# Causal 16-head attention: second passes laid out by halves of the queries

## The reference, cut to what matters

```
x = x + _L1_attn_ref(_layernorm(x), W_Q, W_K, W_V, W_O)

B, S, _ = x.shape                                  # 4, 1024
Q, K, V = (proj(W_Q), proj(W_K), proj(W_V))        # (B, 16, S, 8): heads of 8
Q = _apply_rope(Q, cos, sin); K = _apply_rope(K, cos, sin)
scores = einsum('bhsd,bhtd->bhst', Q, K) / sqrt(8)
scores = where(tril(ones((S, S))), scores, -inf)   # causal
out = einsum('bhst,bhtd->bhsd', softmax(scores), V)
return einsum('bsd,ed->bse', out.transpose(0, 2, 1, 3).reshape(B, S, 128), W_O)
```

## Time and profile before

| | |
|---|---|
| median of three runs | 5018.72 us |
| profiled execution, own time | 5018.88 us |
| its span, first to last instruction | 5017.5 us |
| PE, DVE, ACT, POOL busy, share of the span | 93%, 86%, 66%, 58% |
| mean granted TensorE clock | 0.969 of 2.4 GHz |
| causal stage, first to last maximum | 3851.6 to 4399.7 us |

### The profile page before, as it was taken

One profiled execution on the slowest core, in us unless ns is written; L12 is line 12 of the kernel. 1 busy time (PEld: TensorE's weight loads), 2 busy tenths in 40 slices (PEclk: granted clock), 3 DMA queues, 4 the chain that ended last, 5 costly groups with the idle time before them and its releaser, 6 DMA issues.

```text
span 5017.5 us, 149633 instructions
## 1 busy us (share of the span) xinstructions
PE 4665.0 (93%) x62728; PEld 3234.6 (64%) x62728; DVE 4324.5 (86%) x8627; ACT 3291.3 (66%) x6490; POOL 2930.2 (58%) x3101
## 2 busy tenths in 40 slices
PE   6999997999999999999999999999996999989978
PEld 3444444777777777777777777777775555545467
DVE  7989997999999999999999999999986777768566
ACT  4888884666666666666666666666663777756632
POOL 1330305778877887788778777877872222016744
PEclk7999998999999999999999999999997999989989
DMA  0000100000000000000000000000000000000000
GB/s 25 2 2 1 34 6 25 23 10 12 13 27 11 12 13 27 10 13 14 26 13 16 13 27 11 12 13 10 8 5 27 2 2 2 2 17 1 1 1 18
DMA packets 51764, 63.72 MB, mean 13 GB/s; under 512 B 12820, under 2 KB 41258, under 8 KB 50322
## 3 DMA queue, kind: packets, MB, share of 16 engines
q1 hardware_dynamic: 51090, 54.14, 3.6%
HBM read 25.17 MB, written 4.19 MB: 6 GB/s over the span
## 4 chain that ended last, share of the span: by engine, by line
PE 54%; DVE 26%; ACT 9%; issue 8%; POOL 3%; DMA 0%; SPq 0%; DVEq 0%; POOLq 0%; ACTq 0%
PE psum L582 7%; PE psum L1182 6%; PE psum L1244 6%; PE psum L551 5%; PE psum L1227 4%; PE psum L1259 3%; DVE a_top L731 3%; PE psum L1191 3%; PE psum L1299 3%; DVE b_cross L1498 3%; DVE b_stat L1537 3%; PE psum L568 2%; DVE x L1531 2%; DVE x L1494 2%; DVE b_prob_t L1550 1%
## 5 line engine op out<-in xcount | busy, mean ns | idle before, releaser
L1651 POOL TENSOR_TENSOR x<-x,b_cross 128x512 f32<-128x512 f32 x768 | 984.4, 1285 | 58.3 <-DVE b_cross L1498 58.3
L1657 POOL TENSOR_TENSOR x<-x,b_norm 128x512 f32<-128x512 f32 x768 | 788.3, 1046 | 206.9 <-ACT b_norm L1338 206.0
L1259 PE MATMUL psum<-b_w_vo,b_mixed 128*128 128x128 f32 x6144 | 779.1, 275 | 0.3 <-issue 0.3
L1259 PEld LDWEIGHTS psum<-b_w_vo,b_mixed 128*128 128x128 f32 x6144 | 753.4, 192 | 26.8 <-issue 0.4
L731 DVE TENSOR_REDUCE a_top<-psum 128x2 f32<-128x1024 f32 x512 | 604.1, 1218 | 64.8 <-PE psum L551 61.1
L665 ACT ACTIVATE a_prob<-psum 128x512 f32<-128x512 f32 x1024 | 543.3, 598 | 60.1 <-PE psum L568 46.3
L1664 POOL TENSOR_TENSOR x<-x,b_stat 128x512 f32<-128x512 f32 x384 | 397.5, 1048 | 309.4 <-DVE b_stat L1542 309.0
L1331 ACT ACTIVATE b_square<-psum 128x512 f32<-128x512 f32 x768 | 462.6, 602 | 143.8 <-PE psum L1182 120.7
L1494 DVE TENSOR_TENSOR x<-psum,b_table 128x512 f32<-128x512 f32 x768 | 515.6, 671 | 16.3 <-ACT b_square L1331 15.6
L1380 ACT COPY b_mixed<-psum 128x512 f32<-128x512 f32 x768 | 439.6, 601 | 137.1 <-PE psum L1244 137.0
L1498 DVE TENSOR_TENSOR b_cross<-psum,b_table 128x512 f32<-128x512 f32 x768 | 521.9, 679 | 0.0
(11 more groups left out here) (354 smaller groups left out, 10678.5 us busy)
## 6 DMA issues: line engine op xcount, KB each, us to landing
b_prev<-b_xs_x SPq DMA_DIRECT2D x24, 384.0 KB
ab<-in_L_ffn_Wqkv SPq DMA_DIRECT2D x6, 1024.0 KB, 5.0
b_shifted_x<-y SPq DMA_DIRECT2D x24, 224.0 KB
b_shifted_f<-y SPq DMA_DIRECT2D x48, 112.0 KB, 2.1
ab<-in_L_ffn_Wqkv SPq DMA_DIRECT2D x6, 512.0 KB, 6.0
ab<-in_L_ffn_Wo SPq DMA_DIRECT2D x6, 512.0 KB, 7.3
b_prev<-b_xs_x SPq DMA_DIRECT2D x24, 112.0 KB
x<-in_L_attn_x SPq DMA_DIRECT2D x4, 512.0 KB, 6.5
```

What stands on the lines that cost most here:

```text
L1259: made = e.matmul(banks[n][:, 0:D], mixed[:, h, :], w_vo[l % 2][:, h, :], start=h == 0, stop=h == 2 * PAIRS - 1)
L1651: e.tensor_tensor(turned, turned, crossing, ALU.add).then_inc(sem["roped"], 1)
L1657: e.tensor_tensor(rh, rh, bcast(norm[i % 2][:, 1, HPC * c:HPC * (c + 1)], 2, LDIM), ALU.mult).then_inc(sem["scaled"], 1)
```

## The change

In the causal stage `parts` becomes CHUNKS = 2, as it is in the other attention stage.

```diff
@@ mha_order
-    parts = 1 if causal else CHUNKS
+    parts = CHUNKS
     each, chunks = TILES // parts, CHUNKS // parts
```

## The result

The changed kernel takes 5083.93 us (median of 4 runs, 5080.39 to 5090.21), the kernel before 5020.4 us on the same chips: a ratio of 1.0133, 95% interval 1.0121 to 1.0145. It is slower by 64 us where 11 us less was forecast, and lies outside the range. The profiled execution, the slowest of the four, took 5090.2 us; its span is 71.1 us longer than before.

The account below looks back on a forecast made before the run. No engine was simply full: in-order PE waits for banks that DVE or ACT hold, the limit varying by slots. Head -1.1, tail -9 and units -1.4 took 5018.9 to 5007.4 us; range 4992 to 5030.

Parts of the forecast that it names:

- that the stage's clock stays as it was: Causal stage's steady units: priced at full granted clock; a fall there was given no size or chance.
- The prediction's own sign of being wrong: Causal stage: wrong if a plain unit is below 31.3 or above 33 us, or the steady clock falls.
- plain unit: 24 causal-stage slots with norms and projections elsewhere: forecast -0.25 us, to 32.05 us.
- Slots 8 to 15, +1.25 us: Second third of each unit: all four seconds groups become 512 wide; 12.0 us, ends 11.4 and 13.6.
- Slots 16 to 23, -1.35: Last third of each unit: narrow groups replace 512-wide ones; 10.05 us in place of 11.42, ends 9.1 and 11.4.
- Slots 0 to 7, -0.15: First third of each unit: same pairs, a turn_q2 leaves and a turn_back comes; -0.15 us.
- Head, -1.1: Start of causal stage: slots 22 to 29 gain seconds beside firsts, 11.0 us in place of 12.1.
- The assumption on the clock: Head: clock rises 9 us after seconds begin, wherever that is; if it stays at 3902.0 instead, +3 us.
- Tail, -9: After the last first: 8 slots of seconds alone drop out; -9 us, ends -13 and -7.
- Shift operations, 0: Each unit: three more on DVE, +0.4 us covered by idle time in slots 8 to 10; uncovered, 6 us.
- The ACT rival: ACT bounds slots 8 to 15 at 13.6 us, plain unit 34.7; slower, 5043 us; chance 0.20.

Follow-up runs that it names:

- e1: Changed kernel, groups of c = 1 reordered to k = 4 to 7, then 0 to 3, restoring the old seconds-to-firsts pairing with the 22-slot lag; 5021.5 us, 1.0017.
- e12: Changed kernel, DVE's 512-column maxima in slots 16 to 23 taken over only the first 256 columns; 5028.74 us, 1.0021.
- e10: e1 with the groups of c = 0 in the order k = 0, 3, 2, 1; 5026.67 us, 1.0014.
- e11: e10 with turn_q2 of the first half at slot 18 in place of 12; 5022.09 us, 1.0007.
- e2: Changed kernel with its halves and two shifts a unit, but seconds back at the old lag of 30 slots; 5021.05 us, 1.0006.
- e3: Changed kernel with the score matmuls of firsts in slots 16, 17, 20, 21 issued twice; 5103.77 us, 1.0158.
- e6: Changed kernel with a whole-array identity transpose ahead of firsts in slots 16, 17, 20, 21 and every other first in slots 0 to 7; 5145.32 us, 1.0249.

## Why the prediction was wrong, by its steps

**The failed step: that the stage's clock stays as it was.** Every term was priced from rows at a grant of 1.00, and the clock was a question only of head and tail. It was named at the end as what would make the prediction wrong ("if the granted clock falls in the steady part") but had no price and no chance. It is some 63 of the 76 us in units 2 to 14, and e1, which puts the old pairing back, regains 56 of the 64. The prediction's own sign of being wrong, a plain unit above 33 us or a fall of the clock, came true in both its parts. The sums of the prediction held the warning: PE's work in slots 16 to 23 was to fall while DVE's 9.1 us stayed, so PE would have less to do there; that was read as a gain. Whether that would cost the clock couldn't be read from rows in which it never fell.

**Slots 8 to 15, +1.25 us.** Right mechanism, sized too small: +1.93, 12.70 us at full clock for 12.0, with ACT busy 11.36 (11.3 by the sum) and PE for all 12.70 where its sum had 11.4. (The upper end, 16 x 0.62 + 6 x 0.59, is 13.5 and not 13.6.)

**Slots 16 to 23, -1.35.** Measured -1.06: 10.36 for 10.05, with DVE busy 9.31.

**Slots 0 to 7, -0.15.** Measured +0.12: 10.23. The plain unit at full clock is thus 33.29, not 32.05, and by itself puts the stage some 14 us over the forecast (the estimate of 13 above, and the 1.4 forecast as a gain). So the kernel would have been about as slow as before even with the clock held.

**Head, -1.1.** Measured +0.4. Slots 0 to 21, where no change was forecast, took 30.9 us for 29.2, at a grant of 0.50 from the start; the rest of units 0 and 1 took 1.3 us less, about the term. The assumption on the clock held in this execution: the first exp came 31.1 us behind the first maximum for 42.2, and the rise 8.0 us behind that exp for 8.2. It was in part luck: with the same lag the rise came 13.2 us behind the first exp in e1, 22.2 in e12 and 30.5 in e10.

**Tail, -9.** Measured -4.7. The clock was at 1.2 GHz for the tail's first 23 us, against 10.2 us in its middle before; slots 384 to 389 alone took 11.6 us for 5.7. The windows of the changed kernel's tail are of slots 384 to 389, 390 to 397 and 398 to 405.

```profile
4476.29:4487.90 11.61, 11.61 (x100) 5.79 (x99) 6.46 (x39) 5.14 (x15) 0.00 (x0) 0.50 0.00 1
4487.90:4499.90 12.00, 11.91 (x58) 3.83 (x58) 7.35 (x42) 8.75 (x17) 0.00 (x0) 0.54 0.00 0
4499.90:4508.00 8.10, 8.10 (x116) 4.52 (x114) 0.69 (x1) 6.00 (x17) 0.00 (x0) 1.00 0.01 2
```

But the term was too large even with the clock up at the start: in e11, where it was, the tail took 40.3 us for 43.6, -3.3. PE reaches the end of the diagonal groups earlier and then stands for DVE for 4.22 us, where before it stood for 1.29:

```profile
4424.79 0.54 PE L567 MATMUL psum<-c_blocks 32*128 32x128 bf16 x9 [4.22 <-DVE c_o L785]
```

DVE runs the norms of the next stage for 13.4 us in both, and takes the next `turn_back` only then; in e11 it even begins them later, 4.2 us behind the last maximum for 1.3, since a `turn_back` now stands ahead of them. The prediction had seen that DVE would be as busy there, and still took most of the 10.1 us for gained.

**Shift operations, 0.** Measured 0.2 us a unit by e2, with the `turn_q2` in PE's full third.

**The ACT rival** had slots 8 to 15 at 13.6 us and a slower kernel, 5043 us. The sign came true, the reason didn't: the third took 12.70 us, and the 63 us of the clock are no part of it.

What stays open is what brings the clock down in slots 1, 7, 8 and 9, with PE busy for 96% or more of the 7 us ahead of some of the falls, and what the chip counts: whether it is columns, rows or the time without a matmul. e3 and e6 added matmuls of two kinds without holding the clock, but both also lengthened the stretch, so neither decides it.

## What to carry to other kernels

Before moving work between stretches of a loop, add up what TensorE itself has in each stretch, not only who bounds it: a stretch that another engine paces and from which TensorE's work is taken can cost the clock of the stretches behind it, here for up to 27 us at a time. Look at the granted clock by unit before looking at waits. In this kernel narrow products held the clock where they lay beside transposes and away from slots in which TensorE stands for a reader of its banks (e10, e11 in units 2 to 14). A lag shorter by 8 slots in 384 was worth nothing measurable in the kernel's time even where the clock held (e11).

## What the runs showed that was not expected

The granted clock falls with PE almost always busy: in the 7 us ahead of each of the changed kernel's fifteen falls it was busy for 84 to 96% and never idle for more than 0.56 us at a time. The Trainium skill (TensorE: Matmul & The Clock Gate, "HAM oscillation — how this bites in real kernels") ties the losses that this section describes to long idle gaps of the PE. The trace doesn't agree: it has no such gap ahead of any of these falls, and the measurement decides. Nor does a busy PE by itself bring the clock back: in units 3, 8, 13 and 14 it stayed at 1.2 GHz through slots 0 to 7, where PE was busy without a break (16.06 of 16.06 us in unit 3), and rose in slot 10, with transposes and 512-wide products. In units 5, 7, 9 and others it rose earlier, in slots 1 to 5. And a single whole-array matmul between 32-row ones cost 0.23 us, where in a run of four it takes 0.15 (0.59 for four).
